# Attention layer with a routed low-rank feed-forward: the router's logits are computed while the LayerNorm tiles are still in SBUF, and the top-2 choice is made ahead of the feed-forward

## The chip, the cores and the metric

The kernel runs on all 8 cores of one Trainium2 chip, as eight independent copies of one program: core c takes half c mod 2 of the tokens of batch c // 2 (2048 tokens, with all 4096 keys of that batch). Nothing is exchanged between cores. The time is device microseconds of the slowest core. A profile shows the span of the slowest core, here core 2.

## The reference

One post-LayerNorm layer: attention, residual and LayerNorm, then a linear layer with eight routed low-rank adapters, residual and LayerNorm. D is 4096.

```python
x = layernorm(x + attention(x))                   # 8 heads of 64, softmax / sqrt(512)
logits  = x @ W_router.T                          # [tokens, 8]
probs   = softmax(logits)
topk_p, topk_i = top_k(probs, 2)
topk_p  = topk_p / sum(topk_p)
combine = sum(one_hot(topk_i, 8) * topk_p[..., None], axis=1)
h       = einsum('nd,erd->ner', x, A_stack) * combine[..., None]     # rank 16
out     = x @ W_base.T + b_base + 2.0 * einsum('ner,eor->no', h, B_stack)
x = layernorm(x + out)
```

## The kernel before

Everything is kept transposed: features on the 128 partitions (32 chunks of 128, called mc or dc in the loops), tokens along the free axis. Each stage is a block of five instruction streams (PE, ACT, DVE, POOL, SP). The order inside each stream is the order in which the Python code calls `s.op`; an engine runs its stream strictly in that order and waits by semaphores for what an operation names in `waits`. Between stages stands `phase_barrier`: the first operation of each engine in the new stage waits for every DMA issued so far. A DMA also waits for the one issued two or three places earlier on the same stream of semaphores ("ld" and "sc" have three each, "sca" and "out" two).

**Stage 3** is attention; its end leaves OT, the attention output. The change doesn't touch it or anything before it.

**Stage 4** (lines 892 to 1076) is the output projection with the first LayerNorm. It works on four token groups (qg) of 512 tokens. For each group, a loop over the 32 chunks mc does: four matmuls into one of three PSUM tiles po0 to po2; on DVE the residual sum `res` (line 981: po plus bias plus xq); on ACT its square `sq` (line 991); and, three chunks late, two matmuls with a column of ones (pstS, pstQ) that gather the sums. After the loop `ln_rows` (lines 277 to 305) turns the sums into a scale row and a shift row on one partition. What is then left of the group is put into a list `opend` of 41 closures: one that broadcasts the two rows with TensorE and copies them to `abc` and `bbc`, 32 "applies" (POOL multiplies `res` by `abc` into one of two tiles tmpf, line 1034; DVE adds `bbc` and writes x2g, line 1044), and a spill of x2g to DRAM (x2scr, line 1057) after each fourth apply. The next group's loop takes 2 closures from the head of that list ahead of each chunk. So the applies of group qg run between the residual sums of group qg + 1, on the same DVE. The last group has no successor: its list is emptied after the loop.

**Stage 5** (lines 1077 to the end) first loads A, B and the router weights through two staging tiles wstgf with casts on POOL (`small_load`, lines 1138 to 1161). Then, for each half th of 1024 tokens:

- SP loads the half from x2scr into x2h in eight pieces of four chunks (line 1204), and behind them, in the loop over wq, the f32 base weights wbT in pieces of 512 KB into wstgf (line 1398); POOL casts each piece to wqf (line 1405), which has two buffers of eight pieces.
- PE: 64 router matmuls into rows 0 to 7 of pf0. DVE copies them to lg8 (line 1234). PE: 64 matmuls with A (`ar_bf`) into the whole of pf0.
- The top-2 part: eight transposes of lg8 through pf1, each with a DVE copy (lines 1259, 1264); softmax, two maxima and masks in fourteen small operations on DVE and one on ACT (lines 1278 to 1343); eight transposes back with DVE casts (lines 1352, 1359); an expansion to 128 rows by two matmuls; DVE copies it to ce (line 1376) and multiplies the A result by it: hs (line 1380).
- The base product: 16 quarters wq of two output chunks. Each output chunk is two sweeps of 32 matmuls over dc (one for each 512 tokens), and each sweep ends with one matmul of B with hs. So the first base matmul, which needs pf0 again, waits for hs.
- After the 32 output chunks a second `ln_rows`, whose rows are broadcast into pf0 and pf1. The outputs of half 0 are applied (lines 1176 to 1196) during the base product of half 1, two for each wq, the DMA and the POOL multiply ahead of that wq's weights. The outputs of half 1 are applied at the very end.

A matmul record carries line 155, the helper `mm`, so its operand names tell which it is.

## Time and profile before

| | |
|---|---|
| the runs shown | 3962.08 and 4112.85 us, median 4037.46 us |
| the profiled execution | 3976.92 us, span of its slowest core 3975.4 us |
| spans of the eight cores | 3903.9 to 3975.4 us |
| TensorE busy | 3210.3 us, 81% of the span |
| VectorE, ScalarE, GpSimd busy | 1305.5, 864.1 and 669.1 us |
| stage 4 | about 2323 to 2681 us of the span |
| stage 5 | 2681 us to the end |

How the rows below are read. A line of the timeline is: start in us, length in us, engine, line of the code, operation, output and inputs with their shapes, how many instructions are merged, and in brackets how long the engine sat idle before it and what released it. SPq and ACTq are DMA issues of these engines. "PEld" is the weight load, which overlaps matmuls. In the table of stretches, each engine has its busy time and its number of instructions, then come the granted TensorE clock (1.00 is 2.4 GHz, 0.50 is 1.2 GHz), the busy share of the DMA engines, and GB/s.

### The profile page before, as it was taken

The page shows a single profiled execution, that of the slowest core. Times are in us where ns is not written, and L with a number is a line of the kernel's source. Part 1 is how long each engine was busy: PE and PEld are TensorE (multiplying, and loading weights), DVE is VectorE, ACT ScalarE, POOL GpSimd, SP SyncE. Part 2 cuts the span into 40 slices and gives each one's busy share as a digit, 9 for nine tenths or more (in the row PEclk, how much of TensorE's full clock was granted, in tenths as well). Part 3 has the DMA queues.
Part 4 walks back from the last instruction along what each step waited for, and adds up shares of the span by engine and source line. Part 5 has one row for each costly group of instructions (what it writes and reads, how often), then busy time and mean ns, then how long its engine had stood idle before and what let it go on. Part 6 is the DMA issues. An engine that isn't in the chain of part 4 may idle for free.

```text
span 3975.4 us, 46436 instructions; the slowest of 8 cores (3903.9 to 3975.4 us)
## 1 busy us (share of the span) xinstructions
PE 3210.3 (81%) x13334; PEld 1188.2 (30%) x13476; DVE 1305.5 (33%) x1972; ACT 864.1 (22%) x1476; POOL 669.1 (17%) x543
## 2 busy tenths in 40 slices
PE   4767699787998899898988886624999998999960
PEld 2555243231222222222212221101444433444420
DVE  1000100125555555556546537861000012111124
ACT  1222100002443434334434442210000000000000
POOL 1111000000000000000000005552222213444425
PEclk7999799885677767758758899966999998999985
DMA  7999644520000000000000023217355435667637
GB/s 222 277 268 274 200 136 137 183 90 6 6 6 4 16 6 1 14 6 6 1 14 6 6 88 101 96 59 223 117 161 154 144 125 189 202 206 209 211 104 203
DMA packets 451794, 444.79 MB, mean 112 GB/s; under 512 B 22624, under 2 KB 403681, under 8 KB 451554
## 3 DMA queue, kind: packets, MB, share of 16 engines
q1 hardware_dynamic: 348642, 341.13, 29.1%
q10 hardware_dynamic: 102912, 100.68, 8.0%
q8 instruction: 124, 2.03, 0.2%
q14 instruction: 116, 0.95, 0.1%
HBM read 340.01 MB, written 100.66 MB: 111 GB/s over the span
## 4 chain that ended last, share of the span: by engine, by line
PE 58%; DVE 8%; issue 4%; DMA 4%; POOL 2%; ACT 1%; SPq 1%; DVEq 0%; POOLq 0%; ACTq 0%
PE pf L155 24%; PE sS L155 11%; PE rb L155 10%; PE a L155 7%; DVE racc L629 4%; DMA outT<-outst 2%; DVE x2g L1044 2%; POOL tmpf L1034 2%; PE po L155 2%; PE sS L654 1%; PE pss L155 1%; DMA wstgf<-wbT 1%; DVE outst L1190 1%; PE psq L155 1%; PE pstS L155 1%
## 5 line engine op out<-in xcount | busy, mean ns | idle before, releaser
L155 PE MATMUL pf<-x2h,wqf 128*128 128x512 bf16 x4018 | 905.7, 381 | 10.5 <-DVE hs L1380 5.8
L629 DVE TENSOR_REDUCE racc<-sS 128x1 f32<-128x512 f32 x1024 | 681.9, 689 | 511.0 <-PE sS L155 500.2
L777 ACT ACTIVATE probs<-rb 128x512 bf16<-128x512 f32 x1024 | 541.2, 597 | 757.9 <-PE rb L155 757.4
L155 PEld LDWEIGHTS pf<-x2h,wqf 128*128 128x128 bf16 x4096 | 396.5, 98 | 505.9 <-issue 39.5
L155 PE MATMUL sS<-kT,qT 64*128 64x512 bf16 x1024 | 483.1, 492 | 74.2 <-DVE racc L629 38.3
L155 PE MATMUL pk<-xbf,wk_bf 128*128 128x256 bf16 x2048 | 273.9, 289 | 146.9 <-ACT xbf L367 57.3
L155 PE MATMUL a<-probs,V 128*65 128x512 bf16 x1024 | 377.8, 496 | 0.0
L1471 DVE SCALAR_TENSOR_TENSOR res2c<-pf,bB_sb,x2h 128x1024 bf16<-128x1024 f32 x64 | 82.2, 1284 | 865.1 <-PE pss L155 807.6
L1405 POOL CAST wqf<-wstgf 128x1024 bf16<-128x1024 f32 x256 | 264.5, 1040 | 589.2 <-DMA wstgf<-wbT 431.6
L155 PE MATMUL rb<-qT,kT 64*128 64x512 bf16 x1024 | 348.1, 485 | 0.2
L589 POOL CAST wo_bf<-wstgo 128x1024 bf16<-128x1024 f32 x16 | 16.6, 1040 | 1749.6 <-DMA wstgo<-woT 1749.6
L1489 ACT ACTIVATE sqc<-res2c 128x1024 bf16<-128x1024 bf16 x64 | 67.6, 1057 | 952.2 <-DVE res2c L1471 923.7
L155 PE MATMUL rb<-mrow,ones 1*128 1x512 bf16 x1024 | 251.9, 478 | 27.8 <-DMA mrow<-mtmp 27.7
L155 PE MATMUL pv<-wv_bf,xvb 128*128 128x512 bf16 x1002 | 240.2, 393 | 40.4 <-DVE wv_bf L238 16.2
L155 PEld LDWEIGHTS pk<-xbf,wk_bf 128*128 128x128 bf16 x2048 | 201.7, 102 | 218.7 <-issue 185.3
L155 PEld LDWEIGHTS sS<-kT,qT 64*128 64x128 bf16 x1024 | 97.7, 96 | 439.6 <-issue 435.4
L1034 POOL TENSOR_TENSOR tmpf<-res,abc 128x512 f32<-128x512 bf16 x128 | 158.5, 1253 | 326.6 <-DVE abc L1015 272.3
L155 PE MATMUL po<-OT,wo_bf 128*128 128x512 bf16 x496 | 137.6, 402 | 73.1 <-DVE res L981 66.2
L1184 POOL TENSOR_TENSOR tmpo<-res2d,a 128x1024 f32<-128x1024 bf16 x64 | 152.9, 2408 | 253.5 <-DMA res2d<-r2scr 107.7
L155 PEld LDWEIGHTS a<-probs,V 128*65 128x65 bf16 x1024 | 109.8, 133 | 182.3 <-issue 161.1
L155 PEld LDWEIGHTS pv<-wv_bf,xvb 128*128 128x128 bf16 x1024 | 98.4, 99 | 181.9 <-issue 76.3
L1044 DVE TENSOR_TENSOR x2g<-tmpf,bbc 128x512 bf16<-128x512 f32 x128 | 141.5, 1136 | 34.0 <-POOL tmpf L1034 33.5
(105 smaller groups left out, 1641.9 us busy)
## 6 DMA issues: line engine op xcount, KB each, us to landing
wstgf<-wbT SPq DMA_DIRECT2D x256, 512.0 KB
xstg<-xrot SPq DMA_DIRECT2D x128, 512.0 KB
xscr<-xbf ACTq DMA_DIRECT2D x128, 256.0 KB, 5.5
xvb<-xscr SPq DMA_DIRECT2D x128, 256.0 KB, 2.7
outT<-outst ACTq DMA_DIRECT2D x64, 512.0 KB, 4.7
xqb<-xscr SPq DMA_DIRECT2D x32, 512.0 KB, 3.6
xq<-xscr SPq DMA_DIRECT2D x32, 512.0 KB, 3.7
x2scr<-x2g ACTq DMA_DIRECT2D x32, 512.0 KB, 2.8
```

Source lines behind the costliest of these rows:

```text
L155: return lambda e: e.matmul(o, l, r, start=st, stop=sp, skip_group_check=True)
L589: srd=wstgo[0][:]: e.tensor_copy(d, srd),
L629: e.reduce_max(d, srd, AX.X, negate=True),
L654: idn=id32[:]: e.transpose(o, i, idn),
L777: e.activation(d, srd, AF.Exp),
L1034: e.tensor_tensor(d, a, b, ALU.mult),
L1044: e.tensor_tensor(d, a, b, ALU.add),
L1184: b=a2[:]: e.tensor_tensor(d, a, b, ALU.mult),
L1190: b=b2[:]: e.tensor_tensor(d, a, b, ALU.add),
L1405: e.tensor_copy(d, srd),
L1471: e.scalar_tensor_tensor(d, a, b, c2, ALU.add, ALU.add),
L1489: e.activation(d, a, AF.Square),
```

## The change

- In stage 4 the router's logits are now computed group by group. The router weights are loaded and cast first (a DMA into tmpf0 ahead of all xq loads, a POOL cast to wr_bf2). After the 41 closures of a group, 33 more are put into `opend`: 32 router matmuls of x2g[mc] into a PSUM tile `prt` and one DVE copy to rlg_sb. The loop takes 3 closures ahead of each chunk instead of 2. At the end of the stage ACT writes rlg_sb (8 x 2048 f32, 64 KB) to DRAM (rlgscr).
- In stage 5 the load of the router weights, both blocks of 64 router matmuls and both lg8 copies are gone. One DMA reads rlgscr into lg8, ahead of the x2h loads. The top-2 part, otherwise unchanged, is now a function that is called for half 0 and then for half 1, ahead of the loop over th, with a ce tile for each half. In the loop stand the x2h loads, the A matmuls, hs and the base product.

```diff
+                tlw = s.op("SP", lambda e: e.dma_start(
+                    tmpf[0].ap().rearrange("p (c n) -> p c n", n=8)[:, 0:32, :],
+                    wrT.ap().rearrange("(c p) n -> p c n", p=128)),
+                    waits=[], dma="ld")
+                tmpfR[0].did_write(tlw)
+                tcw = s.op("POOL", lambda e: e.tensor_copy(wr_bf2[:],
+                                                           tmpf[0][:, 0:256]),
+                           waits=[tlw])
...
                         for mc in range(NDC):
-                            for _ in range(2):
+                            for _ in range(3):
                                 if opend:
                                     opend.pop(0)()
...
+                        for mc in range(NDC):
+                            def mk_rtr(qg=qg, mc=mc):
+                                def f():
+                                    t = s.op("PE", mm(
+                                        prt.ap()[0:8, 0:512],
+                                        wr_bf2[:, mc * 8: mc * 8 + 8],
+                                        x2g[:, mc * 512: mc * 512 + 512],
+                                        mc == 0, mc == NDC - 1),
+                                        waits=x2gR[mc].rd() + wrR2.rd() +
+                                        (prtR.wr() if mc == 0 else []),
+                                        tok=(mc == NDC - 1))
...
+                            opend.append(mk_rtr())
+                        def mk_revac(qg=qg):
+                            def f():
+                                t = s.op("DVE",
+                                         lambda e,
+                                         d=rlg_sb[:, qg * 512: qg * 512 + 512],
+                                         srd=prt.ap()[0:8, 0:512]:
+                                         e.tensor_copy(d, srd),
+                                         waits=prtR.rd())
...
+                        opend.append(mk_revac())
                     while opend:
                         opend.pop(0)()
+                    s.op("ACT", lambda e: e.dma_start(rlgscr.ap(), rlg_sb[:]),
+                         waits=list(rlg_toks), dma="sca")
...
-            small_load(wr_bf, wrR,
-                       wrT.ap().rearrange("(c p) n -> p c n", p=128), 8)
...
-                for th in range(2):
-                    for g in range(8):
-                        tl = s.op("SP", lambda e, th=th, g=g: e.dma_start(
...
-                    for dc in range(NDC):
-                        for sub in range(2):
-                            last = s.op("PE", mm(
-                                pf[0].ap()[0:8, sub * 512: sub * 512 + 512],
-                                wr_bf[:, dc * 8: dc * 8 + 8],
...
-                    tlg = s.op("DVE", lambda e, d=lg8[:],
-                               srd=pf[0].ap()[0:8, 0:1024]:
-                               e.tensor_copy(d, srd), waits=[last] + lg8R.wr())
...
+                tlg8 = s.op("SP", lambda e: e.dma_start(
+                    lg8[:], rlgscr.ap()), waits=[], dma="ld")
+                lg8R.did_write(tlg8)
+
+                def emit_top2(th):
                     for qc in range(8):
                         tt = s.op("PE",
                                   lambda e, o=pf[1].ap()[0:128, 0:8],
-                                  i=lg8[:, qc * 128: qc * 128 + 128],
+                                  i=lg8[:, th * 1024 + qc * 128:
+                                        th * 1024 + qc * 128 + 128],
...
+                emit_top2(0)
+                emit_top2(1)
+                for th in range(2):
+                    for g in range(8):
+                        tl = s.op("SP", lambda e, th=th, g=g: e.dma_start(
...
+                    for dc in range(NDC):
+                        for sub in range(2):
+                            last = s.op("PE", mm(
+                                pf[0][:, sub * 512: sub * 512 + 512],
+                                ar_bf[:, dc * 128: dc * 128 + 128],
...
+                    ths = s.op("DVE",
+                               lambda e, d=hs[:], a=pf[0][:], b=ce2[th][:]:
                                e.tensor_tensor(d, a, b, ALU.mult),
```

## Rows read from the trace of the kernel before

**Rows 1.** The page: the span, busy time by engine, the chain that ended last

```profile
span 3975.4 us, 46436 instructions; the slowest of 8 cores (3903.9 to 3975.4 us)
...
PE 58%; DVE 8%; issue 4%; DMA 4%; POOL 2%; ACT 1%; SPq 1%; DVEq 0%; POOLq 0%; ACTq 0%
```

**Rows 2.** Stretches of stages 4 and 5: us, busy by engine, clock, DMA share

```profile
2386.00:2445.00 59.00, 37.30 (x132) 10.29 (x134) 52.01 (x57) 13.22 (x22) 39.44 (x32) 0.94 0.30 99
...
2721.00:2735.00 14.00, 9.52 (x41) 3.16 (x40) 0.00 (x0) 0.00 (x0) 1.02 (x1) 1.00 0.95 360
...
2753.00:2778.00 25.00, 5.54 (x17) 1.91 (x17) 10.18 (x32) 1.54 (x2) 8.87 (x9) 0.54 0.68 203
```

**Rows 3.** Timeline, stage 4 while the applies of group 0 run: residual sums and multiplies

```profile
2390.66 0.74 DVE L981 SCALAR_TENSOR_TENSOR res<-po,bo_sb,xq 128x512 bf16<-128x512 f32 x1
...
2401.35 2.53 POOL L1034 TENSOR_TENSOR tmpf<-res,abc 128x512 f32<-128x512 bf16 x2 [0.75 <-DVE x2g L1044]
...
2404.36 0.74 DVE L981 SCALAR_TENSOR_TENSOR res<-po,bo_sb,xq 128x512 bf16<-128x512 f32 x1
2404.64 1.16 POOL L1034 TENSOR_TENSOR tmpf<-res,abc 128x512 f32<-128x512 bf16 x1 [0.75 <-DVE x2g L1044]
...
2406.55 2.53 POOL L1034 TENSOR_TENSOR tmpf<-res,abc 128x512 f32<-128x512 bf16 x2 [0.75 <-DVE x2g L1044]
```

**Rows 4.** Timeline, stage 4 after the last applies of group 0: residual sums

```profile
2446.35 0.75 DVE L981 SCALAR_TENSOR_TENSOR res<-po,bo_sb,xq 128x512 bf16<-128x512 f32 x1 [0.74 <-PE po L155]
...
2458.30 0.75 DVE L981 SCALAR_TENSOR_TENSOR res<-po,bo_sb,xq 128x512 bf16<-128x512 f32 x1 [0.74 <-PE po L155]
```

**Rows 5.** Timeline, end of stage 4: first and last adds of group 3's 32 applies

```profile
2626.87 1.75 DVE L1044 TENSOR_TENSOR x2g<-tmpf,bbc 128x512 bf16<-128x512 f32 x2 [0.17 <-DVE bbc L1020]
...
2675.70 2.16 DVE L1044 TENSOR_TENSOR x2g<-tmpf,bbc 128x512 bf16<-128x512 f32 x2 [1.12 <-POOL tmpf L1034]
```

**Rows 6.** Timeline, start of stage 4: the first xq issue and the first residual sums

```profile
2325.48 18.41 SPq L925 DMA_DIRECT2D xq<-xscr  x10
...
2331.91 2.89 DVE L981 SCALAR_TENSOR_TENSOR res<-po,bo_sb,xq 128x512 bf16<-128x512 f32 x4 [9.65 <-DMA xq<-xscr]
```

**Rows 7.** Timeline, start of stage 5: SP's DMA issues

```profile
2680.91 8.38 SPq L1145 DMA_DIRECT2D wstgf<-aallT  x4
...
2693.03 8.71 SPq L1145 DMA_DIRECT2D wstgf<-ballT  x4
...
2704.86 0.38 SPq L1145 DMA_DIRECT2D wstgf<-wrT  x1
```

**Rows 8.** DMA, 2704 to 2712 us in 40 slices of 0.2 us: GB/s in each

```profile
GB/s 307 164 164 184 184 205 225 82 61 36 61 47 41 34 33 30 24 25 41 61 80 69 59 37 7 94 44 25 155 215 348 379 369 420 399 399 369 369 399 399
```

**Rows 9.** Timeline, half 0: A matmuls, first transpose, eighth cast, first base sweep

```profile
2736.93 15.45 PE L155 MATMUL pf<-x2h,ar_bf 128*128 128x512 bf16 x62 [2.33 <-DVE lg L1234]
...
2752.30 0.22 PE L1259 MATMUL pf<-id,lg 8*128 8x8 f32 x1
2752.45 1.04 POOL L1405 CAST wqf<-wstgf 128x1024 bf16<-128x1024 f32 x1 [1.69 <-DMA wstgf<-wbT]
...
2778.25 9.04 PE L155 MATMUL pf<-x2h,wqf 128*128 128x512 bf16 x31 [2.91 <-DVE hs L1380]
```

**Rows 10.** Timeline, half 1 of stage 5: router, A, top-2, base; the eighth cast

```profile
3286.74 16.00 PE L155 MATMUL pf<-x2h,wr_bf 128*8 128x512 bf16 x64
...
3304.53 13.76 PE L155 MATMUL pf<-x2h,ar_bf 128*128 128x512 bf16 x62 [1.78 <-DVE lg L1234]
...
3318.22 0.22 PE L1259 MATMUL pf<-id,lg 8*128 8x8 f32 x1
3318.25 1.04 POOL L1405 CAST wqf<-wstgf 128x1024 bf16<-128x1024 f32 x1 [2.58 <-DMA wstgf<-wbT]
...
3338.19 1.22 DVE L1376 CAST ce<-pf 128x1024 bf16<-128x1024 f32 x1 [1.36 <-PE pf L155]
...
3340.99 9.27 PE L155 MATMUL pf<-x2h,wqf 128*128 128x512 bf16 x31 [2.91 <-DVE hs L1380]
```

More of the change, by code:

```diff
@@ L1092, in build_program @@
             brR = Res()
-            wr_bf = sbP("wr_bf", [128, 32 * 8], BF16)
-            wrR = Res()
             hs = sbP("hs", [128, 1024], BF16)
             hsR = Res()
-            ce = sbP("ce", [128, 1024], BF16)
-            ceR = Res()
+            ce2 = [sbP("ce%d" % i, [128, 1024], BF16) for i in range(2)]
+            ceR2 = [Res(), Res()]
             lgt = sbP("lgt", [128, 64], F32)
@@ L1114, in build_program @@
             cmTR = Res()
-            lg8 = sbP("lg8", [8, 1024], F32)
+            lg8 = sbP("lg8", [8, 2048], F32)
             lg8R = Res()
```

96 lines of the change are left out of this document (47 added, 49 removed).

## The prediction

> **What bounds the kernel now.** I read the page first: the chain that ended last is TensorE for 58% of the span and DVE for 8% [rows 1]. The change touches only stages 4 and 5, so the question is which wait ends last there. Stage 4 has three regimes. While the applies of the previous group run, the residual sums on DVE stand 2.74 us apart: from 2390.66 to 2404.36 are 5 steps in 13.70 us, and they hold 8 applies, because 10 closures are taken in 5 chunks and 2 of them are spills [rows 3]. The pace is that of the applies: POOL waits 0.75 us for the DVE add before each pair [rows 3], and with nothing between them, after the last group, the applies run hardly faster: 32 from 2626.87 to 2677.86 (2675.70 + 2.16) [rows 5], 1.6 us each. A POOL pair takes 3.29 us to the next multiply (2401.35 to 2404.64), a lone one 1.91 (2404.64 to 2406.55) [rows 3]. So an apply costs 13.70 / 8 = 1.71 us with the sums between, 1.64 at best. Once the list is empty, sums come every 1.494 us (8 steps from 2446.35 to 2458.30), released by po: TensorE paces [rows 4]. After the last group only the applies run. In stage 5 TensorE is full inside the base product; what is open are the two heads of the halves, from the x2h load to the first base sweep [rows 9, 10].
>
> **Stage 4, the start.** The router weights go ahead of the xq loads. Their pieces are 32 bytes, 4096 of them. In stage 5 the same load is issued at 2704.86 and moves little: for some 18 of the 0.2 us slices the queue moves under 95 GB/s, then 350 to 420 [rows 7, 8]. The first sum waits for xq, issued at 2325.48, until 2331.91 [rows 6]. I take 3.5 us more, on the path, since TensorE then paces group 0; the bounds are 0.4 (the issue alone [rows 7]) and 4.0. The POOL cast lies in time in which POOL has nothing to do; uncovered it would cost at most 1.04 us, what a cast of four times its size takes [rows 10].
>
> **Stage 4, three closures instead of two.** It sounds harmless and is the largest term. The applies can't go faster, their pace is their own. With 2 closures for each chunk the 41 closures span 20.5 chunks, with 3 only 13.67. So 6.83 chunks of projection, which ran in the applies' shadow, move behind it, where a chunk costs 1.494 us [rows 4]: 10.2 us for a group. The apply stretch itself: I take 1.70 us for each, between 1.71 and 1.64 with fewer sums in between, 0.4 us less. The 33 router closures follow. A block of 64 matmuls of 512 columns takes 13.76 us at full clock (two of its records are missing), 0.215 us each [rows 10]. TensorE may run three chunks ahead of DVE (three po tiles), so the matmuls put ahead of chunks 13 to 16, ten of them, fall into its waits; 22 x 0.215 = 4.7 us are added where it paces. The copy of prt (0.75 us at most, as a sum [rows 4]) fits in DVE's 0.74 us gaps, and what waits behind it is one residual sum with three po tiles of slack. Together 10.2 - 0.4 + 4.7 = 14.5 us for each of the three groups with a successor: **43.5 us**. Below: applies at 1.64 (-2.3) and all router matmuls hidden, 7.9 x 3 = 24. Above: each apply as the lone one at 2404.64, whose successor starts 1.91 us later [rows 3], +6.3; no matmul hidden, 6.9; 23.4 x 3 = 70.
>
> On the pace of the applies the Trainium skill (SBUF — State Buffer, "SBUF: two separate sides") says that DVE with two SBUF inputs and GpSimd exclude each other for whole instructions. By it fewer sums in between would buy the applies nothing, the 0.4 us above fall away and the sum is 1.2 us higher; the trace, with 1.71 against 1.64, shows a little give.
>
> **Stage 4, the end.** The last router matmul waits for the last add (2677.86), then comes the copy, then the 64 KB write, which the barrier waits for. Before, the last spill went out right behind the add. One half-clock matmul 0.43 us (16.00 - 13.76 shows the half-clock start [rows 10]), the copy 0.75, three hand-overs: **+1.6 us**, bounds 0.8 and 2.5.
>
> **Stage 5, half 0.** Before: SP's first load 2680.91, base start 2778.25 [rows 7, 9]. After: the fourth B load is issued at 2701.4 as before, lg8 right behind it at 2701.7; I let it land at 2706 (as long as the B load ahead of it; 2704.5 to 2709). Then TensorE's stream has the top-2 part twice, ahead of the A matmuls, so it can't use x2h however early that arrives. One top-2 part is 3338.19 - 3318.22 = 20.0 us to the ce copy, 21.3 with it, since the next one needs pf1 [rows 10]. Half 0's was 3.2 us longer (25.95 against 22.77 us from first transpose to base [rows 9, 10]), of which I keep 1.3 (a table load). So 22.6 + 20.0 = 42.6: the A matmuls begin at 2748.6, take 16.0 [rows 10], hs and its hand-overs 1.6 (2.80 us from ce to base less ce's 1.22 [rows 10]): base at 2766.2, 12.0 us earlier. The eighth cast of the first weights, at 2752.45, is done by then [rows 9]. And the sweep begins at full clock: a gap of 1.78 us ahead of the A matmuls kept it (62 in 13.76), where a long idle one did not (64 in 16.00) [rows 10]; 2.2 us. Together **-14.2 us**, bounds 10 and 18.
>
> **Stage 5, half 1.** The router matmuls, the copy and the top-2 part leave the path: the A matmuls start at 3286.74 in place of the router's, hs is done 16.0 + 1.6 us later at 3304.3, base could start there and not at 3340.99 [rows 10]: 36.7 us. But a sweep needs all eight pieces of weights, and the eighth cast ends at 3319.29 [rows 10], on DMA. x2h, res2d and wbT are queued as before, so it stays there. The sweep ends at 3320.3 instead of 3350.3; that is 30.0, less 2.2 for a half-clock restart after trickling matmuls: **-27.8 us**, bounds 24 and 30. Next late would be the second set of weights; POOL's next multiplies waited for DVE adds that stood behind hs, and hs is now early, so I cost them at nothing; the lower bound of 24 is for them.
>
> **Sum** against the profiled execution's 3976.92 us: 3.5 + 43.5 + 1.6 - 14.2 - 27.8 = +6.6, so 3983.5. All ends together give -23 to +43. The median of the runs shown, 4037.46, is 60 us above the profiled execution, the two runs being 151 apart; a like median of the changed kernel may stand that much above the sum too.
>
> **Rivals.** *The projection stays hidden* (faster): if TensorE's lead or a faster apply pace absorbs the displaced chunks, stage 4 costs only its two ends, 5 us, and the total is 5 - 42 = -37, 3940. For it: TensorE sits idle for a third of the apply stretch (37.30 us busy of 59.00 [rows 2]). Against: its lead is only three tiles, and the adds go in order with the sums. Chance 0.13.
>
> *TensorE falls to half clock in the apply stretch* (slower): a chunk's work is spread over 4.0 us instead of 2.74, so its busy share falls from 0.63 to about 0.45. Rows at 0.63 to 0.68 busy have 0.94 and 1.00 of the clock, one at 0.22 has 0.54 [rows 2]. Each group would then restart slowly, 2.2 x 3 = 6.6 us, and with applies at 1.91 us, 70 + 6.6: 77 us in stage 4, total +40, 4017. The Trainium skill (TensorE: Matmul & The Clock Gate, "HAM oscillation") warns of just such bursts with idle between; by its rule alone the sum would be 3990. Chance 0.20. It would take 79 us, that is 26 us more for a group than I forecast, to be slower by 2%: 0.05.
>
> *The heads don't shrink*: lg8 lands late or the second top-2 part delays the A matmuls beyond 2764; then half 0 gives nothing, 3998. In my range, with the forecast's 0.62.
>
> **Chances.** Forecast with its own range 3954 to 4012: 0.62; hidden projection 0.13; slower pace 0.20; beyond 2% slower 0.04, beyond 2% faster 0.01, for which more than the whole of the removed head work would have to vanish at no cost in stage 4. About 2% is what a measurement of this kernel tells from no change. The range goes from 3942 to 4062: the lower end at the hidden projection, the upper at the slower pace, with the offset of a median like the one shown.
>
> **What would show it.** Group period (abc copy to abc copy) up from 79 to about 94 us; sums 1.5 us apart from chunk 17 on, with router matmuls between; first xq wait 3 us longer; base of half 0 some 12 us sooner after SP's first load; half 1's first sweep trickling with the casts. A period near 80 would make the prediction wrong downwards; one over 105 upwards.

## The result, and the profile after

The changed kernel is slower, by less than the 2% that a short measurement tells apart, but clearly: 34 runs of the kernel before have a median of 3971.7 us (3932.0 to 4250.3), 35 of the changed one 3994.57 us (3956.1 to 4289.1). In some runs the cores of one half of the chip take several per cent longer at a lower clock, whatever the kernel; the ratio of the others is 1.0061, with a 95% interval of 1.004 to 1.0083, so about +24 us (16 to 33). The prediction said +6.6. The time lies in its range, but that range is 120 us wide and so bears out little; the shift does not agree with its sum.

The profiled execution of the changed kernel took 3975.62 us, less than the 3976.92 of the one before. That isn't a gain. Both the start of stage 4 and the time behind the last matmul scatter over tens of us from core to core, so two single spans can't be subtracted. What can be compared is one step of the work at a time, as the median of the eight cores of each profiled execution. Each event counts from its start; a difference of 0.1 us is rounding:

| step (median of 8 cores, us) | before | after | difference | predicted |
|---|---|---|---|---|
| last `OT` write to first xq issue | 4.5 | 5.0 | +0.5 | +3.5 with the next |
| first xq issue to first residual sum | 6.2 | 8.0 | +1.8 | |
| stage 4, `abc` copy of group 0 to that of group 3 | 238.0 | 286.1 | +48.1 | +43.5 |
| `abc` copy of group 3 to the last `x2g` add | 52.9 | 52.9 | 0 | 0 |
| last `x2g` add to SP's first load of stage 5 | 3.7 | 4.9 | +1.2 | +1.6 |
| that load to the first `res2c` of half 0 | 113.9 | 103.5 | -10.4 | -14.2 |
| first `res2c` to half 0's copy of `a` | 488.7 | 489.0 | +0.3 | 0 |
| half 0's copy of `a` to the last `res2c` of half 1 | 547.6 | 526.1 | -21.5 | -27.8 |
| sum | | | +20.0 | +6.6 |

The sum of the steps, +20.0, lies inside the measured 16 to 33. Every step for which a change was forecast went the way that the prediction said. The three large ones came out worse, by 4.6, 3.8 and 6.3 us, the two small ones together 1.6 us better. Two stretches are left out of the sum: the start, up to the end of attention (median 2288.6 us before, 2307.7 after, while its code is the same; over all twelve kernels of this study the medians lie between 2286 and 2312), and the end, from half 1's copy of `a` to the last output add (117.7 and 104.5), whose scatter has a section below.

First the stretch that cost most. The windows of the changed kernel, its slowest core (7): us; busy time of TensorE matmuls, weight loads, DVE, ACT and POOL with their counts; granted clock, DMA share, GB/s. The first line is the time in which group 0's applies run, the second what is left of the group:

```profile
2378.00:2434.00 56.00, 35.42 (x96) 8.47 (x95) 45.39 (x48) 8.20 (x13) 39.87 (x32) 0.74 0.28 94
2434.00:2473.00 39.00, 34.91 (x135) 10.35 (x134) 17.96 (x26) 13.35 (x21) 0.00 (x0) 0.94 0.26 82
```

Before, the line that answers to the first has 132 matmuls in 59 us at a clock of 0.94 [rows 2]; now 96 in 56 us at 0.74. The 32 multiplies of POOL take their old time, and fewer chunks of the projection fit beside them.

The timeline of the same core shows both rhythms. Start, duration, engine, line, operation, idle time before it and what ended it:

```profile
2400.16 0.74 DVE L999 SCALAR_TENSOR_TENSOR res<-po,bo_sb,xq 128x512 bf16<-128x512 f32 x1
...
2402.36 2.54 POOL L1052 TENSOR_TENSOR tmpf<-res,abc 128x512 f32<-128x512 bf16 x2 [0.75 <-DVE x2g L1062]
...
2420.43 0.74 DVE L999 SCALAR_TENSOR_TENSOR res<-po,bo_sb,xq 128x512 bf16<-128x512 f32 x1
...
2432.87 0.67 DVE L1062 TENSOR_TENSOR x2g<-tmpf,bbc 128x512 bf16<-128x512 f32 x1
...
2439.94 0.75 DVE L999 SCALAR_TENSOR_TENSOR res<-po,bo_sb,xq 128x512 bf16<-128x512 f32 x1 [1.32 <-PE po L155]
2440.19 0.81 PE L155 MATMUL prt<-x2g,wr_bf 128*8 128x512 bf16 x3
...
2442.08 0.75 DVE L999 SCALAR_TENSOR_TENSOR res<-po,bo_sb,xq 128x512 bf16<-128x512 f32 x1 [1.39 <-PE po L155]
```

From 2400.16 to 2420.43 are five steps of the residual sum, 4.05 us each, where there were 2.74 before [rows 3]. The multiplies wait for the same DVE add as before. The group's 32 applies run from 2379.1 (start of the first multiply) to 2433.54 (2432.87 + 0.67), 1.70 us each, as the prediction took it. Behind them the sums stand 2.14 us apart with three router matmuls in each step: 1.494 + 3 x 0.215 is 2.14.

Why can't the applies go faster? The prediction took their pace from the rows. One multiply of the same core and the add that starts beside it, timeline:

```profile
2407.03 1.16 POOL L1052 TENSOR_TENSOR tmpf<-res,abc 128x512 f32<-128x512 bf16 x1
...
2407.18 1.56 DVE L1062 TENSOR_TENSOR x2g<-tmpf,bbc 128x512 bf16<-128x512 f32 x1 [0.46 <-POOL tmpf L1052]
```

The add takes 1.56 us here and 0.67 us where no multiply runs: it ends 0.54 us behind the multiply's end. In the same way a multiply takes 1.41 us in place of 1.16 when it starts beside the end of an add. The residual sum, which reads PSUM and only one large SBUF tile, keeps its 0.74 us beside a multiply. So in these rows a multiply on POOL and an add of two SBUF tiles on DVE run one after the other, although they are on two engines, and two multiplies and two adds together make the 3.29 us of a pair. Fewer sums between them leave that nearly as it is.

The granted clock of 0.74 is a mean. Two windows of the same stretch, columns as above:

```profile
2391.70:2398.40 6.70, 5.56 (x12) 1.03 (x12) 5.40 (x7) 1.26 (x2) 4.93 (x4) 0.50 0.47 157
...
2405.40:2412.00 6.60, 2.19 (x9) 0.49 (x8) 5.02 (x7) 0.63 (x1) 5.07 (x4) 1.00 0.22 79
```

TensorE goes back and forth between 1.2 and 2.4 GHz while the applies run.

The head of half 0, same kernel and core, timeline. SP's first load of the stage, the issue of `lg`, the first transpose of either top-2 part, the A matmuls, the first base sweep:

```profile
2721.38 7.74 SPq L1193 DMA_DIRECT2D wstgf<-aallT  x4
...
2741.26 0.45 SPq L1248 DMA_DIRECT2D lg<-rlgscr  x1
...
2747.53 0.24 PE L1258 MATMUL pf<-id,lg 8*128 8x8 f32 x1 [29.68 <-DMA lg<-rlgscr]
...
2771.50 0.24 PE L1258 MATMUL pf<-id,lg 8*128 8x8 f32 x1 [1.58 <-DVE ce L1375]
...
2792.62 16.54 PE L155 MATMUL pf<-x2h,ar_bf 128*128 128x512 bf16 x64
...
2810.85 7.07 PE L155 MATMUL pf<-x2h,wqf 128*128 128x512 bf16 x32 [1.69 <-DVE hs L1414]
```

The base starts 89.5 us after SP's first load, before it was 97.3 [rows 7, 9]: 7.9 us sooner, not 12.0. The sweep of 32 takes 7.07 us; before, 31 matmuls took 9.04 [rows 9]. So the start at full clock came about, and with it 2.0 to 2.2 us.

The head of half 1, same core:

```profile
3314.12 1.23 DVE L1556 COPY a<-pf 128x1024 f32<-128x1024 f32 x1 [1.93 <-PE pf L155]
...
3325.18 30.51 SPq L1432 DMA_DIRECT2D wstgf<-wbT  x8
3333.47 1.22 DVE L1414 TENSOR_TENSOR hs<-pf,ce 128x1024 bf16<-128x1024 f32 x1 [14.71 <-PE pf L155]
...
3334.77 4.97 DVE L1236 TENSOR_TENSOR outst<-tmpo,b 128x1024 f32<-128x1024 f32 x2
...
3336.62 4.02 POOL L1439 CAST wqf<-wstgf 128x1024 bf16<-128x1024 f32 x2
...
3338.81 3.84 PE L155 MATMUL pf<-x2h,wqf 128*128 128x512 bf16 x8 [5.45 <-POOL wqf L1439]
...
3346.11 1.86 PE L155 MATMUL pf<-x2h,wqf 128*128 128x512 bf16 x4 [3.46 <-POOL wqf L1439]
...
3361.16 1.04 POOL L1439 CAST wqf<-wstgf 128x1024 bf16<-128x1024 f32 x1 [2.34 <-DMA wstgf<-wbT]
```

`hs` begins 19.3 us after the copy of `a` (median of the cores 19.6, before 55.9): the router matmuls and the top-2 part are off the path. But the first sweep trickles in fours with the casts. The eighth cast ends at 3362.20, which is 48.1 us after the copy; the median of the cores is 42.0 (38.1 to 48.1), before it was 36.5 (35.2 to 42.3). In the waits of this core for the whole of half 1 the casts hold TensorE up for 15.8 us in 7 waits, all in this first sweep.

### The profile page after: what moved, and what is told of

Same layout as the page of the kernel before. It is cut to its first block, busy times and chain, and to the rows that moved or that the text cites. A ratio compares the mean times of both kernels' runs of the same rounds, so it can differ in the third digit from the quotient of the medians.

```text
span 3974.1 us, 46631 instructions; the slowest of 8 cores (3923.9 to 3974.1 us)
## 1 busy us (share of the span) xinstructions
PE 3246.1 (82%) x13476; PEld 1187.5 (30%) x13476; DVE 1306.9 (33%) x1974; ACT 863.6 (22%) x1476; POOL 666.4 (17%) x543
## 4 chain that ended last, share of the span: by engine, by line
PE 58%; DVE 8%; issue 4%; DMA 4%; POOL 3%; ACT 0%; SPq 0%; DVEq 0%; POOLq 0%; ACTq 0%
PE pf L155 24%; PE sS L155 11%; PE rb L155 9%; PE a L155 7%; DVE racc L630 4%; PE po L155 2%; DVE x2g L1062 2%; POOL tmpf L1052 2%; DMA outT<-outst 1%; PE sS L655 1%; PE pss L155 1%; PE pstS L155 1%; DMA x2h<-x2scr 1%; DVE outst L1236 1%; DMA wstgf<-wbT 1%
## 5 line engine op out<-in xcount | busy, mean ns | idle before, releaser
L155 PE MATMUL pf<-x2h,wqf 128*128 128x512 bf16 x4096 | 915.1, 382 | 17.6 <-POOL wqf L1439 15.8
L155 PE MATMUL a<-probs,V 128*65 128x512 bf16 x1024 | 369.1, 486 | 0.0
L155 PE MATMUL po<-OT,wo_bf 128*128 128x512 bf16 x512 | 160.7, 450 | 75.0 <-DVE res L999 69.2
```

The lines of the kernel that those rows point to most:

```text
L155: return lambda e: e.matmul(o, l, r, start=st, stop=sp, skip_group_check=True)
```

## Experiments

Three costs were in doubt: what of the 48.1 us in stage 4 belongs to the three closures and what to the router matmuls (A, against the rival that the matmuls or a falling clock carry it), what holds half 1 back (C, the casts and what their loads share the DMA queues with), and what half 0 still waits for (E, the top-2 part of half 1, which stands ahead of the A matmuls). The table has the steps of all runs as medians of eight cores, in us; a group is one of the three with a successor. The eighth cast of half 1 (its end) and the last `res2c` are counted from half 0's copy of `a`; the column between them is the time from the first to the eighth cast. Of e1, e2, e5 and e9 too few whole runs are comparable for a ratio, so they are read by their steps alone.

| kernel | group | first load to first `res2c` | eighth cast | first to eighth | last `res2c` |
|---|---|---|---|---|---|
| before | 79.3 | 113.9 | 36.5 | 19.4 | 547.6 |
| changed | 95.4 | 103.5 | 42.0 | 23.3 | 526.1 |
| e1, before with three closures | 90.3 | 113.1 | 36.5 | 20.9 | 547.7 |
| e2, changed, two closures, router in pairs | 83.9 | 103.0 | 40.0 | 22.2 | 524.5 |
| e3, changed, two closures, router inside the applies | 79.3 | 102.6 | 38.6 | 22.6 | 522.6 |
| e4, changed, first weights ahead of the output applies | 95.6 | 103.1 | 34.2 | 20.4 | 528.7 |
| e5, changed, no top-2 part of half 1 | 95.2 | 81.7 | 42.2 | 24.0 | 526.0 |
| e6, e3 with three staging tiles | 78.8 | 104.6 | 36.4 | 18.3 | 519.8 |
| e7, e3, no output applies in two quarters | 79.3 | 103.9 | 32.4 | 19.1 | 600.6 |
| e8, e3, A matmuls between the top-2 steps | 79.3 | 89.7 | 41.1 | 22.9 | 525.3 |
| e9, e8, output applies behind each quarter's weights | 79.0 | 88.5 | 34.8 | 20.3 | 518.3 |
| e10, e9, three staging tiles, later router load | 78.9 | 87.5 | 32.1 | 16.1 | 516.4 |

**The three closures alone.** In the kernel before, with nothing else changed:

```diff
-                            for _ in range(2):
+                            for _ in range(3):
                                 if opend:
                                     opend.pop(0)()
```

> The kernel before with one edit: three closures of the list are taken ahead of each chunk of stage 4 instead of two. No router matmul is moved. Theory A (displaced chunks): the applies keep their pace, 6.83 chunks fall out of their shadow, so the time from one abc copy to the next grows from 79.3 us to about 89.5 us, or 90.8 if the half clock in the apply stretch costs its 1.3 us, and the whole kernel becomes about 31 to 35 us slower, ratio 1.008 to 1.009. Rival B (it is the router's 32 matmuls and their waits that lengthen a group, and three closures are harmless): the period stays under 82 us and the ratio within 0.998 to 1.002. On the clock: if the half clock comes from spreading the chunks' work over the applies, the granted clock of the apply stretch falls from 0.94 to about 0.74 here too; if it comes from the router matmuls it stays at 0.94.

The period of a group went from 79.3 to 90.3 us: 11.0 us, with no router matmul in stage 4. All other steps stayed. So two thirds of the 16.0 us that a group lost (95.4 - 79.3, the medians rounded) come from one digit. The windows of its slowest core, the apply stretch and what follows it:

```profile
2389.00:2445.00 56.00, 32.15 (x88) 7.35 (x88) 45.36 (x48) 8.10 (x13) 39.90 (x32) 0.77 0.28 94
2445.00:2479.00 34.00, 29.92 (x110) 8.07 (x109) 17.59 (x25) 13.39 (x22) 0.00 (x0) 0.90 0.29 93
```

The mean clock falls here too, to 0.77, with no router matmul in stage 4, so it goes with the thinner projection and not with the router matmuls. What that costs is seen in the timeline where the applies end:

```profile
2446.35 0.75 DVE L981 SCALAR_TENSOR_TENSOR res<-po,bo_sb,xq 128x512 bf16<-128x512 f32 x1 [0.18 <-PE po L155]
2448.78 0.75 DVE L981 SCALAR_TENSOR_TENSOR res<-po,bo_sb,xq 128x512 bf16<-128x512 f32 x1 [1.68 <-PE po L155]
2450.21 0.75 DVE L981 SCALAR_TENSOR_TENSOR res<-po,bo_sb,xq 128x512 bf16<-128x512 f32 x1 [0.68 <-PE po L155]
```

One step of 2.43 us, then the usual pace. Against 1.494 that is 0.9 us for the group; the granted clock is 0.50 from 2444.80 to 2448.00 and 1.00 behind it. Displaced chunks at 9.8 us and this restart make 10.7 of the 11.0.

**Router matmuls in pairs, two closures.** The changed kernel, with as many closures for a chunk as before and one closure for two router matmuls:

```diff
-                            for _ in range(3):
+                            for _ in range(2):
...
-                        for mc in range(NDC):
-                            def mk_rtr(qg=qg, mc=mc):
+                        for m2 in range(0, NDC, 2):
+                            def mk_rtr(qg=qg, m2=m2):
                                 def f():
+                                    for mc in (m2, m2 + 1):
```

> The changed kernel, but with two closures ahead of each chunk again, and the router matmuls put into the list in pairs (16 closures in place of 32) so that the list is empty before the next group. Theory A: the apply stretch again covers 20.5 chunks; of the 32 router matmuls, four ahead of each chunk, those in TensorE's lead of three chunks are hidden and some 20 x 0.215 = 4 us are added: period 83 to 84 us against 95.1 in the changed kernel, about 34 us less in three groups, ratio to the kernel before 0.996 to 0.999. Rival B: the period stays at 93 to 95 us and the ratio at 1.006.

83.9 us for a group. The 11.0 us are gone, and what stays over the 79.3 of before is 4.6, the router matmuls behind the applies, where TensorE paces. The remaining question was whether they could be hidden as well.

**A router matmul ahead of each apply.** Two closures, and the matmul for chunk `mc - 8` at the head of the closure of apply `mc`; the last eight follow in four closures:

```diff
                             def mk_apply(mc=mc, rtr=rtr):
                                 def f():
+                                    if mc >= 8:
+                                        rtr(mc - 8)
...
+                        for mc in range(NDC - 8, NDC, 2):
+                                    rtr(mc)
+                                    rtr(mc + 1)
```

> The changed kernel with two closures ahead of each chunk, and each router matmul put into the closure of the apply eight chunks later, so that 24 of the 32 run while TensorE waits for the residual sums anyway; the last eight follow in four closures. Theory A: these 24 cost nothing and the last eight fall into TensorE's lead: period 79.5 to 81 us, 43 to 46 us less than the changed kernel in three groups, ratio to the kernel before 0.993 to 0.996. Rival B (a matmul that waits for an apply takes TensorE's lead away from the projection): the period is 85 us or more and the gain under 30 us.

79.3 us: the router costs nothing there. The window of its slowest core:

```profile
2396.00:2452.00 56.00, 42.54 (x160) 12.13 (x158) 49.78 (x54) 11.97 (x19) 39.51 (x32) 0.95 0.32 104
```

160 matmuls in 56 us at a clock of 0.95. TensorE has room beside the applies, and filled with work it keeps its clock. The ratio to the kernel before is 0.9889 (0.9826 to 0.9953), some 44 us faster (19 to 69). This is the idea of the change without its loss in stage 4.

**The first weights of half 1 ahead of the output applies.** In the changed kernel:

```diff
-                        for _ in range(2):
+                        for _ in range(0 if wq == 0 else 2):
                             if apply_pend:
                                 emit_apply(*apply_pend.pop(0))
...
+                        for _ in range(2 if wq == 0 else 0):
+                            if apply_pend:
+                                emit_apply(*apply_pend.pop(0))
```

> The changed kernel with one edit in stage 5: for the first quarter of a half the two output applies (their res2d loads on SP and their multiplies on POOL) are issued behind the eight weight pieces instead of ahead of them. Theory C (in the changed kernel half 1's first base sweep waits for the eighth weight cast, and the res2d loads and the two multiplies are what delays it beyond the x2h transfer): the eighth cast ends 8 to 12 us sooner after the a copy than the 42 us (median of the cores) of the changed kernel, and the time from hs of half 1 to the last res2c falls from 506 us to about 497; total about 9 us less than the changed kernel, ratio to the kernel before about 1.004. Rival D (DMA bandwidth alone sets it, the order doesn't matter): the eighth cast moves by 3 us or less and the total by no more.

The eighth cast came 7.8 us sooner, at 34.2, and nothing was won: the last `res2c` stands at 528.7 us, against 526.1. The ratio to the kernel before is 1.0048 (1.0004 to 1.0092), no better than what it started from as far as can be told. The timeline of its slowest core (2) shows where the time went:

```profile
3368.13 4.24 POOL L1230 TENSOR_TENSOR tmpo<-res2d,a 128x1024 f32<-128x1024 bf16 x2
...
3373.65 2.93 POOL L1230 TENSOR_TENSOR tmpo<-res2d,a 128x1024 f32<-128x1024 bf16 x1 [1.28 <-DVE outst L1236]
3377.31 2.15 POOL L1230 TENSOR_TENSOR tmpo<-res2d,a 128x1024 f32<-128x1024 bf16 x1 [0.73 <-DMA res2d<-r2scr]
...
3403.08 1.86 PE L155 MATMUL pf<-x2h,wqf 128*128 128x512 bf16 x4 [4.42 <-POOL wqf L1439]
...
3410.12 1.86 PE L155 MATMUL pf<-x2h,wqf 128*128 128x512 bf16 x4 [5.17 <-POOL wqf L1439]
```

The two multiplies left out of the first quarter now stand with those of the second, four in a row between the two sets of casts, and TensorE waits for the second set instead. The reason was half right: the place of the multiplies sets the casts. A wait moved to the next quarter is not a wait removed.

**No top-2 part of half 1.** The changed kernel without `emit_top2(1)`; half 1 takes half 0's `ce`, so its outputs are weighted with the wrong experts:

```diff
-                emit_top2(1)
...
-                               lambda e, d=hs[:], a=pf[0][:], b=ce2[th][:]:
+                               lambda e, d=hs[:], a=pf[0][:], b=ce2[0][:]:
```

> The changed kernel without the top-2 part of half 1: half 1 uses the ce tile of half 0, so half 1's low-rank part of the output is weighted wrongly and 20 us of work are left out. Theory E (in half 0 the second top-2 part stands in TensorE's stream ahead of the A matmuls and is the reason why half 0 gained 10.5 us only): the time from SP's first load of stage 5 to the first A matmul falls from 71 us to 48 to 50 us, and to the first res2c from 103 us to 85 to 88 us, where the eighth weight cast takes over. Rival F (the x2h transfer or the weights bound the head of half 0 anyway): the first res2c comes 98 us or more after SP's first load.

First load to first `res2c`: 81.7 us, 21.8 less than in the changed kernel. That is also below the 85 to 88 expected: the eighth cast hardly holds the sweep up. The whole of the second part, 2771.50 to 2792.62 in the timeline above (21.1 us), lies on the path of half 0. On that core x2h is complete 53.1 us after SP's first load, and the A matmuls begin at 71.2.

**Three staging tiles for the weights,** on e3:

```diff
-            wstg = [sbP("wstgf%d" % i, [128, 1024], F32) for i in range(2)]
+            wstg = [sbP("wstgf%d" % i, [128, 1024], F32) for i in range(3)]
...
-                            st_i = g4 % 2
+                            st_i = wcnt[0] % 3
```

> The kernel of the third experiment (router matmul behind each apply) with three staging tiles for the weights instead of two. Theory G (a weight piece of 512 KB every 2.7 to 2.9 us is the pace of two transfers in flight, not of the DMA bandwidth): pieces come every 2.0 to 2.2 us where nothing else moves, half 1's eighth cast ends 33 to 35 us after the a copy instead of 39, and hs to last res2c falls from 502.7 to about 498 us; total 4 to 5 us less than the third experiment. Rival D (bandwidth): the eighth cast moves by less than 1.5 us and hs to last res2c by no more.

The eighth cast comes at 36.4 in place of 38.6 and the last `res2c` 2.8 us sooner (519.8 against 522.6). That is in the direction expected and less than expected. The eight casts take 18.3 us in place of 22.6, but the first load is issued 2.0 us later behind the copy of `a` than in e3 (7.0 and 5.0, medians), which the third tile doesn't explain. In whole runs (ratio 0.9941, 0.9893 to 0.9989, beside e3's 0.9889, 0.9826 to 0.9953) it can't be told from e3.

**No output applies in the first two quarters,** on e3, three in each of the next four, to see what half 1 would be without them:

```diff
-                        for _ in range(2):
+                        for _ in range(0 if wq < 2 else 3 if wq < 6 else 2):
```

> The kernel of the third experiment, and the output applies of half 0 start only with the third quarter of half 1 (three for each of quarters 2 to 5, two after that). Theory C2 (moving the applies behind the first quarter's weights only handed their delay to the second quarter's, which waited 9.6 us in the fourth experiment): now neither quarter waits beyond its own pieces, the eighth cast ends at 33 to 35 us and hs to last res2c falls from 502.7 us to 496 to 498 us; total 5 to 7 us less than the third experiment, ratio to the kernel before 0.9875. Rival H (the applies are due work, and three in a quarter make a later one wait instead): hs to last res2c stays at 501 us or more.

The eighth cast is at 32.4, 6.2 us sooner than in e3, and the half took 78 us longer (600.6 against 522.6; ratio 1.0129, 1.0049 to 1.0208). Three applies are too many for the two tiles of `tmpo`. The timeline of its slowest core (0), in half 1:

```profile
3313.65 4.23 POOL L1236 TENSOR_TENSOR tmpo<-res2d,a 128x1024 f32<-128x1024 bf16 x2
...
3343.33 1.28 DVE L1511 SCALAR_TENSOR_TENSOR res2c<-pf,bB_sb,x2h 128x1024 bf16<-128x1024 f32 x1 [14.02 <-PE pss L155]
3344.53 2.35 DVE L1242 TENSOR_TENSOR outst<-tmpo,b 128x1024 f32<-128x1024 f32 x2
3345.95 2.92 POOL L1236 TENSOR_TENSOR tmpo<-res2d,a 128x1024 f32<-128x1024 bf16 x1 [28.06 <-DVE outst L1242]
...
3348.82 3.01 POOL L1445 CAST wqf<-wstgf 128x1024 bf16<-128x1024 f32 x2
```

The third multiply waits 28.06 us for an add that stands on DVE behind a residual sum of the quarter before, the casts stand behind the multiply on POOL, and TensorE behind the casts (6.03 us until 3349.99). So it says nothing of how half 1 ends without applies, and much of the queues: POOL's casts are only as free as what is queued ahead of them. One number of it bears on the question: with no apply in the first quarter the eight casts take 19.1 us, as in the kernel before (19.4), and not 22.6 as in e3.

**A matmuls between the steps of the top-2 parts,** on e3. The x2h loads of half 0 are issued ahead of the top-2 parts, and the A matmuls of half 0 are handed out two at a time wherever TensorE would wait for DVE; `hs` of half 0 is emitted inside the second part:

```diff
+                        if th == 1:
+                            fill(1)
...
+                    fill(8 if th else 4)
...
+                        fill(1)
+                        if alast and th == 1 and qc == 5:
+                            emit_hs(0, alast[0])
```

> The kernel of the third experiment, with the A matmuls of half 0 put between the steps of the two top-2 parts, where TensorE waits for DVE, instead of behind them; hs of half 0 is computed in the second part. Theory E: the two parts and the A matmuls overlap, the first res2c comes 86 to 90 us after SP's first load of stage 5 instead of 103, total 13 to 17 us less than the third experiment, ratio to the kernel before about 0.985. Rival I (the steps are lengthened by the matmuls between them, at half clock 0.86 us in a step of 0.76, or a matmul waits for its x2h piece and holds the next transpose): the first res2c comes at 97 us or later.

First load to first `res2c` fell from 102.6 to 89.7 us; of the 16 us of A matmuls some 13 are hidden. In the timeline of its slowest core (6), inside the second part:

```profile
2714.64 0.20 PE L1318 MATMUL pf<-id,lg 8*128 8x8 f32 x1
2714.77 0.60 PE L155 MATMUL pf<-x2h,ar_bf 128*128 128x512 bf16 x2
2715.36 0.19 PE L1318 MATMUL pf<-id,lg 8*128 8x8 f32 x1
...
2719.09 4.06 PE L155 MATMUL pf<-x2h,ar_bf 128*128 128x512 bf16 x18
```

The transposes stand 0.72 us apart with two A matmuls between them. The ratio to the kernel before is 0.9875 (0.9807 to 0.9943).

**Output applies behind each quarter's weights,** on e8, so that the multiplies move behind the casts in every quarter and not only in the first:

```diff
-                        for _ in range(2):
-                            if apply_pend:
-                                emit_apply(*apply_pend.pop(0))
...
+                        for _ in range(2):
+                            if apply_pend:
+                                emit_apply(*apply_pend.pop(0))
```

> The kernel of the eighth experiment (A matmuls between the transposes, router matmul behind each apply), and in every quarter of the base product the two output applies stand behind the eight weight pieces instead of ahead of them, so that there are never more than two applies between two sets of weights. Theory C3 (the fourth experiment lost its gain only because four applies then stood ahead of the second set, the seventh because a third multiply on POOL waits for a DVE add that is queued behind a residual sum): the eighth cast of half 1 ends at 33 to 35 us after the a copy and the a copy to the last res2c falls from 525.3 to 517 to 520 us; ratio to the kernel before 0.984 to 0.987. Rival D (the delay is DMA time and comes back in the second quarter whatever the order): a copy to last res2c stays at 523 us or more.

The eighth cast is at 34.8 in place of e8's 41.1, the last `res2c` at 518.3 in place of 525.3: 7.0 us, which e4 didn't give. No four multiplies come together now. Two things make up the 6.3 us of the cast. The first cast comes 3.7 us sooner: SP no longer issues two `res2d` loads ahead of the weights, so that the first `wbT` issue lies 1.3 us ahead of the copy of `a` (median) and 5.5 us behind it in e8, and no multiply stands ahead of the cast on POOL. And the eight casts take 20.3 us, not 22.9.

**All of it together:** e9, three staging tiles, and the router weights' load moved behind group 0's xq loads.

> The kernel of the ninth experiment with three staging tiles for the weights, and with the load of the router weights in stage 4 behind the eight xq loads of group 0 instead of ahead of them. The three tiles take another 2 to 4 us off the way from the a copy to the last res2c (515 to 518 us). The router load: the theory of the forecast (its small pieces hold up xq) expects the first residual sum 6.2 us after the first xq issue instead of 7.6 and the OT to xq gap back at 4.6 from 5.1, 1.9 us in all; the rival (the slower first sum is noise) expects 7.5 us. Ratio to the kernel before 0.982 to 0.986.

The first residual sum comes 5.8 us after the first xq issue, as before the change (6.2; the changed kernel 8.0), and that issue 4.5 us after the last `OT` write (5.0). So the load ahead of xq costs 2 to 3 us (the first residual sum comes 6.9 to 8.0 us after the issue in the nine kernels that have the load ahead, 5.8 to 6.2 in the other three), and nothing once it stands behind. The head of half 1 in the timeline of its slowest core (7):

```profile
3259.52 24.23 SPq L1467 DMA_DIRECT2D wstgf<-wbT  x8
3281.51 5.62 PE L155 MATMUL pf<-x2h,wqf 128*128 128x512 bf16 x24 [1.69 <-DVE hs L1269]
...
3291.44 1.31 PE L155 MATMUL pf<-x2h,wqf 128*128 128x512 bf16 x4 [2.35 <-POOL wqf L1474]
```

Six of the eight pieces are there soon enough for 24 matmuls to run in one go; the last two still make TensorE wait. The ratio to the kernel before is 0.9867 (0.983 to 0.9904): about 53 us faster (38 to 68). Its steps give -58 (start -0.4, groups -1.2, end of stage 4 +1.2, half 0 -26.4, half 1 -31.2). Put against the changed kernel through its 1.0061, it is some 2% ahead of it. By the steps it is the best of the versions that ran; whole runs can't tell it from e8 (0.9875) or e3.

## Why the prediction was off, step by step

The mechanism held in the main: stage 4 lost by displaced chunks, both heads of stage 5 shrank, and none of the rivals came about as it was priced. What failed is the size of three terms, and in half 1 one link of the mechanism, that the casts stay where they were. An effect of about +20 us is the small rest of +52 and -32, and the three large terms, each off by 10 to 27% and all to the same side, made it three times what was forecast. That all three lie on one side is chance as far as these runs show; each has its own cause.

- **Start of stage 4, +3.5.** Measured +2.3. The router load delays xq, but by less than the slow slices of stage 5 had made it look (21 of them are under 95 GB/s in [rows 8], not 18, which is 4.2 us); e10, where it stands behind xq, has these 2.3 us and a little more back.
- **Three closures, +9.8 for a group.** Measured 11.0 (e1). The 6.83 displaced chunks and the 1.70 us for an apply were right: 32 applies from 2379.1 to 2433.54. The step that failed is the chunk at 1.494 us from the first one on. The prediction had named the falling clock as a rival only, with 2.2 us and slower applies (its line that 79 us would be 26 more for a group than forecast should say 24); the mean clock did fall, from 0.94 to 0.74, the applies kept their pace, and the price was one slow step of 0.9 us. It belonged in the sum, at that size; 0.3 us of the 11.0 aren't explained. The Trainium skill (TensorE: Matmul & The Clock Gate, "HAM oscillation") speaks of a clock that falls again and again where bursts of matmuls alternate with waits. The windows at 0.50 and 1.00 above agree with it in kind, and the one step of 2.43 us is what it cost here.
- **Router matmuls, +4.7 for a group.** Measured 4.6 (e2) to 5.1 (95.4 - 90.3). The 22 of 32 on TensorE's paced stretch, 0.215 us each, fit that.
- **End of stage 4, +1.6.** Measured +1.2.
- **Half 0, -14.2.** Measured -10.4. On the slowest core: `lg` was issued 19.9 us after the first load (20.8 forecast) and needed 6.27 us to the first transpose (2741.26 to 2747.53) where 4.3 was taken, as if it were as quick as the B load ahead of it; the two top-2 parts took 24.0 and 21.1 us, 45.1 in place of 42.6; A and `hs` 18.2 in place of 17.6. That is 2.0 + 2.5 + 0.6 less 0.9, 4.2 us, which takes the -12.0 for the base start to the measured -7.9. The top-2 parts had been read in [rows 10], right behind 128 long matmuls, where a transpose takes 0.22 us; here TensorE had been idle for 29.68 us, and it takes 0.24. But that makes only 0.2 us for each part. In the first, which came out 1.4 us longer than forecast, the rest is the table load, of which 1.3 us had been kept and which costs 1.7 (from the first reduction to the exp 2.36 us, 0.64 without it), the first DVE copy, which comes 0.57 us later behind its transpose, and the hand-overs. In the second, 1.1 us longer, two of the fifteen small DVE operations last 0.62 and 1.00 us in place of 0.23 and 0.16. One of them in the timeline, and the same operation in the kernel before, half 1 (core 2):

```profile
2781.27 1.04 POOL L1439 CAST wqf<-wstgf 128x1024 bf16<-128x1024 f32 x1 [2.88 <-DMA wstgf<-wbT]
2781.32 1.00 DVE L1328 TENSOR_TENSOR stt<-stt 128x8 f32<-128x8 f32 x1
```

```profile
3327.53 0.16 DVE L1329 TENSOR_TENSOR stt<-stt 128x8 f32<-128x8 f32 x1
```

It waits for the cast. In the twelve profiled executions 107 operations of the top-2 parts that write `lg`, `mskb` or `cmb` from SBUF tiles start while a weight cast has at least 0.3 us to run, and every one of them ends 0.07 to 0.08 us behind the cast; the reductions and the copies out of PSUM beside the casts keep their 0.22, 0.17 and 0.28 us. It is what holds the applies of stage 4 apart. So the steps that failed are two: a duration read where POOL had one cast was put where it has seven, and `lg` was given the time of another load. The rival that the heads don't shrink was wrong.
- **Half 1, -27.8.** Measured -21.5, the largest miss. "x2h, res2d and wbT are queued as before, so it stays there" is the sentence that failed. They are queued as before, and the eighth cast still came 5.5 us later (median 42.0 in place of 36.5). The eight casts take longer, 23.3 us in place of 19.4. With two staging tiles they take 22.2 to 24.0 in all five kernels in which `hs` is early and the output applies stand ahead of the weights (changed, e2, e3, e5, e8), 19.4 and 20.9 where `hs` is late (before, e1), and 19.1 to 20.4 where no apply stands ahead (e4, e7, e9). In the kernel before, the `res2d` loads and the multiplies of the first quarter stood there too, but their adds waited on DVE behind an `hs` at 55.9 us; now it is at 19.6, and the adds and the writes of 1 MB behind them run beside the weight loads. The traces show both at work. A weight load of this set, from the third on, stands 4.7 us from its issue to its cast where no write of the output is under way (median of 340 loads, ten kernels with two tiles) and 5.9 where one is for more than half of that time (115 loads); in the changed kernel alone 4.4 and 5.8, in the kernel before 4.7. And the adds hold up the casts themselves: above, two casts take 4.02 us beside two adds, where a cast takes 1.04; on the eight cores that is 0 to 2.0 us, median 0.5. No run held the writes or the adds back alone, so how the 3.9 us divide between them stays open. The rest, 1.6 us, goes with the first `wbT` issue (7.4 us behind the copy of `a` in place of 5.4), which lies between 4.9 and 7.4 in kernels with the same queue there and isn't put down to the change.
- **The rest.** 5.5 of the 6.3 us by which half 1 missed are the casts; 0.8 isn't explained. The base product of half 0 took 0.3 us more (489.0 for 488.7), which wasn't looked into.
- **Projection stays hidden** (-37): wrong; TensorE's three tiles of lead don't carry 6.8 chunks. **Slower pace** (+40): half of it was seen, the clock, and not the other, a slower pace of the applies.

Of the signs that were to decide, the period of a group, 95.4 where 94 was written and 79 was before, came out at once. The sums 1.5 us apart from chunk 17 on are 2.14 while router matmuls stand between them, and then 1.49.

## What to carry to other kernels

When a list of small jobs is drained beside a loop, the number of jobs taken for a turn is a price and not only an order: if their own pace sets the stretch, taking more for a turn leaves less of the loop in their shadow, and what is displaced comes back at full price (11.0 us for a group here, by one digit). Work that is moved into a gap should stand in the gap's order, one item behind each job that it depends on (79.3 us with 32 more matmuls), and work that TensorE has ready should go between the steps of a chain that waits for DVE (some 13 us). A duration of a DVE operation that reads two SBUF tiles holds only for what POOL does beside it: read it where the other engine is as busy as it will be (0.16 us became 1.00). Before an engine's wait is priced away, look at what sets the next release: `hs` of half 1 came 36.4 us sooner and the half ended only 21.5 us sooner. Of these 15 us the prediction had seen 9, the wait for the eighth cast and a restart at half clock; 5.5 more came because that cast itself moved, beside the work that the early `hs` had set free.

## What was not expected of the hardware

The time from half 1's copy of `a`, which stands right behind the last matmuls, to the last output add goes by pairs of cores, and in some executions it takes two values. In the profiled execution of e5 it is 101.5 and 101.6 us on cores 0 and 1, 131.3 and 130.4 on 2 and 3, 101.1 and 101.3 on 4 and 5, 132.0 and 130.1 on 6 and 7. In that of e10 the slow pairs are 0 with 1 (128.1, 130.3) and 6 with 7 (128.2, 129.4), the other four lie at 101.0 to 101.5. The work is the same on all. The same 80 us on cores 1 and 2 of e5, columns as above:

```profile
3840.00:3920.00 80.00, 0.00 (x0) 0.00 (x0) 49.23 (x27) 0.00 (x0) 60.67 (x26) 0.50 0.69 253
```

```profile
3840.00:3920.00 80.00, 0.00 (x0) 0.00 (x0) 27.64 (x18) 0.00 (x0) 41.59 (x18) 0.50 0.84 173
```

Core 1 moves 253 GB/s at a DMA share of 0.69, core 2 173 GB/s at 0.84: its DMA engines are busier and move less. The waits of the two in this time, core 1 and then core 2 (us in total, times, longest):

```profile
DVE outst L1236 <- DMA outT<-outst: 28.5, 12, 2.7
POOL tmpo L1230 <- DMA res2d<-r2scr: 19.9, 13, 1.9
```

```profile
DVE outst L1236 <- DMA outT<-outst: 54.0, 18, 4.6
POOL tmpo L1230 <- DMA res2d<-r2scr: 38.4, 9, 4.9
```

Both the writes of the output and the reads of the residual take twice as much of the engines' waiting. Which pairs are slow changes from one execution to the next and not with the kernel: in the changed kernel's profiled execution none was (101.3 to 110.1), in the one before two were (122.9 to 131.9). The two cores of a pair also work on the same batch, so these runs can't tell a grouping of the chip from one of the program, and what makes a pair slow was not found. It is worth some 28 us, as much as all that this study was about. That is why steps of the same work were compared here and no two spans, and why a kernel that is 24 us slower can show a profiled execution that is faster.

The second surprise is how cheap a falling clock was. Over 56 us of the group shown TensorE changed between 1.2 and 2.4 GHz, 0.74 in the mean, and in e1, with 0.77, that cost one slow step of 0.9 us, because TensorE was not what the stretch waited for; e3 put 32 more matmuls and the displaced chunks into the same 56 us, and the clock was 0.95.
